# Attention stage of a four-stage block: x tiles asked for two tiles ahead, pair loops written out as eight straight-line tiles

## What is computed

```python
x = _layernorm(hidden_states)                       # (8, 1024, 256)
q, k, v = (x @ W.T + b for each of q, k, v)          # 16 heads of 16
attn_scores = einsum('bihd,bjhd->bhij', q, k) / 4
logits = (x @ rel_W[:, :256].T)[:, :, None] + (x @ rel_W[:, 256:].T)[:, None] + rel_b
bias = einsum('bijk,hk->bhij', softmax(logits), logical_bias)
attn_scores += sigmoid(x @ gate_W.T + gate_b) * bias
out = softmax(attn_scores) @ v
hidden_states + out @ Wo.T + bo
```

## Time and profile before

| | us |
|---|---|
| median of 3 runs | 6223.31 (6222.27 to 6227.41) |
| profiled execution, its own time | 6220.41 |
| its span, first to last instruction | 6218.6 |
| attention, from the first head's step of tile 0 to the last of tile 63 | 2943.24 |

### The profile page before, as it was taken

One profiled execution on the slowest core, in us unless ns is written; L12 is line 12 of the kernel. 1 busy time (PEld: TensorE's weight loads), 2 busy tenths in 40 slices (PEclk: granted clock), 3 DMA queues, 4 the chain that ended last, 5 costly groups with the idle time before them and its releaser, 6 DMA issues. The chain is left out here.

```text
span 6218.6 us, 125297 instructions
## 1 busy us (share of the span) xinstructions
PE 5465.2 (88%) x40162; PEld 3538.9 (57%) x40162; DVE 4684.7 (75%) x6099; ACT 4429.8 (71%) x7069; POOL 3649.6 (59%) x2010
## 2 busy tenths in 40 slices
PE   6888888888888888888699969999999979999999
PEld 4666666666666666655444435555555546666665
DVE  7888889889888888888799849999999952221221
ACT  5999989899898998999566668888888841111111
POOL 4777777777777777777300029999999950000000
PEclk8999999999999999999899979999999999999999
DMA  2121121211212121120155565555555541111110
GB/s 71 28 47 29 27 47 30 45 27 29 46 27 47 28 42 31 28 44 17 38 182 193 207 216 182 195 202 200 205 196 198 183 148 34 34 50 34 34 34 11
DMA packets 461188, 538.63 MB, mean 87 GB/s; under 512 B 237520, under 2 KB 337616, under 8 KB 460640
## 3 DMA queue, kind: packets, MB, share of 16 engines
q1 hardware_dynamic: 460640, 531.62, 27.4%
HBM read 370.17 MB, written 161.35 MB: 85 GB/s over the span
## 5 line engine op out<-in xcount | busy, mean ns | idle before, releaser
L502 DVE CUSTOM_DVE_ANT_0 srow<-srow,ps_s,cur 128x1024 f32<-128x1024 f32 x1024 | 1305.5, 1275 | 249.5 <-PE ps_s L650 174.9
L579 ACT ACTIVATE srow<-srow,nmax 128x1024 f32<-128x1024 f32 x1024 | 1192.1, 1164 | 201.5 <-DVE nmax L502 189.7
L588 ACT COPY AT<-ps_t 128x512 f32<-128x512 f32 x2048 | 1105.5, 598 | 61.6 <-PE ps_t L661 60.7
L661 PEld LDWEIGHTS ps_t<-ident,srow 128*128 128x128 f32 x8192 | 959.9, 143 | 279.5 <-ACT AT L588 87.8
L661 PE MATMUL ps_t<-ident,srow 128*128 128x128 f32 x8192 | 1102.5, 278 | 12.6 <-ACT AT L588 8.4
L1977 POOL TENSOR_TENSOR c_hc<-c_hs,c_cs 128x1024 f32<-128x1024 f32 x432 | 1009.9, 2366 | 64.7 <-DVE c_hs L2079 62.6
L491 DVE SCALAR_TENSOR_TENSOR srow<-ps_p,rho,R 128x1024 f32<-128x1024 f32 x768 | 976.7, 1272 | 7.8 <-PE ps_t L661 4.5
L650 PE MATMUL ps_s<-K,Q 96*128 96x512 bf16 x2048 | 629.2, 389 | 402.0 <-DVE nmax L502 313.9
L1938 PE MATMUL c_ps_y<-c_hc,c_ident 128*128 128x512 f32 x2048 | 944.7, 594 | 30.0 <-POOL c_hc L1977 17.1
L2079 DVE TENSOR_TENSOR_SCAN c_hs<-c_da,c_pd 128x1024 f32<-128x1024 f32 x384 | 859.7, 2274 | 56.3 <-PE c_pd L1929 55.1
L2022 ACT ACTIVATE c_sT<-c_dxT,c_bT 128x256 f32<-128x256 f32 x1536 | 668.4, 494 | 108.9 <-PE c_pd L1929 98.7
(11 more groups left out here) (257 smaller groups left out, 8258.3 us busy)
## 6 DMA issues: line engine op xcount, KB each, us to landing
c_cs<-bc_d SPq DMA_DIRECT2D x256, 512.0 KB, 4.3
c_bs<-bc_d SPq DMA_DIRECT2D x64, 512.0 KB, 6.6
Q<-parts_d SPq DMA_DIRECT2D x384, 64.0 KB, 2.2
parts_d<-parts SPq DMA_DIRECT2D x57, 384.0 KB, 3.3
K<-parts_d SPq DMA_DIRECT2D x168, 128.0 KB, 4.3
sz_d<-b_sz SPq DMA_DIRECT2D x16, 1024.0 KB, 7.2
xv_d<-b_xv SPq DMA_DIRECT2D x16, 1024.0 KB, 8.5
dt_d<-b_ab SPq DMA_DIRECT2D x16, 1024.0 KB, 4.2
```

Source lines behind the costliest of these rows:

```text
L502: nc.vector.tensor_tensor_reduce(r[:], r[:], ps_s[:], cur[k][:, h:h + 1], BIG, ALU.add, ALU.min, nmax[:, h % NROW:h % NROW + 1]).then_inc( ...
L579: nc.scalar.activation(r[:], r[:], ACT.Exp, scale=-1.0, bias=nmax[:, h % NROW:h % NROW + 1]).then_inc(e_ok, 1)
L588: nc.scalar.copy(AT[h % NAT][:, HG * half:HG * half + HG, :], ps_t[:, half]).then_inc(at_ok, 1)
L661: last = nc.tensor.transpose(ps_t[:, half, i, :], rows_sb[h % NROW][:, j * P:(j + 1) * P], ident[:])
```

## The change

SP asks for x tile t+10 in tile t instead of t+9, into the other slot, and one more tile (9) ahead of the first `body`. The last loads wrap round to tiles that nobody reads, one more than before, and a wait at the end covers it. In `run`, the two kinds of inner `Fori` become Python loops, so that the instructions of all eight tiles of a batch stand one after the other. The outer loop stays.

```diff
@@ run
-                with eng.Fori(1, NT // 2 - ends) as i:
+                for i in range(1, NT // 2 - ends):
                     for k in range(2):
                         body(eng, first + 2 * i + k, k, par, 2 * i + k, True, True, True, before=par)
...
-            with eng.Fori(1, NT // 2 - 1) as i:
+            for i in range(1, NT // 2 - 1):
                 for k in range(2):
                     body(eng, (B - 1) * NT + 2 * i + k, k, 1, 2 * i + k, False, True, True, before=1)
@@ block.sync
                 sp_first_keys(sp, 1)
                 sp_parts(sp, NT)
+                sp_x(sp, NT + 1, 1)
...
                 if pro:
-                    sp_x(sp, t + AHEAD, 1 - k)
+                    sp_x(sp, t + AHEAD + 1, k)
...
                 sp.wait_ge(st, 16 * TILES)
+                sp.wait_ge(x_in_s, 16 * (TILES + 2))
```

## The result

The change brings the median from 6223.6 us (four executions, one more than in the table of before) to 6144.65; the ratio is 0.9871, with a 95% interval of 0.9858 to 0.9885. One of the four executions after took 7937.86 us, at a mean granted clock of 0.648, and is in the median but not in the ratio; the other three took 6141.94 to 6145.12 us at 0.978 to 0.979. The profiled execution took 6144.19 us, against 6220.41 before.

A forecast was written before the change was run, and what follows sets the result against it. DVE and ACT nearly fill a regular attention tile (45.08 us), so only longer tiles' excess can go: 49.2 (x load) + 18.8 (inner loops) = 68.0 off 6220.4 gives 6152.4; median 2.9 above, 6155; range 6146 to 6180.

The forecast's parts named there:

- The x load: First tiles of batches 1 to 6: asking earlier removes DVE's six waits for x and gains 49.2 us.
- The 1.0 us left for tiles 24 and 40: Part of the 50.2 us excess not counted as gain, since the outer jump's stall and clock dip stay there.
- The inner jumps: 15 tiles behind an inner jump: writing the loops out removes their 22.1 us of excess.
- Rival (b): PE's stall comes at code boundaries anyhow, so writing loops out does not remove it: 6177, chance 0.05.
- the price of that can be read: Engines beside PE fetching straight code: 0.28 us in each of 12 more tiles, a cost of 3.3 us.
- the first two rows of the table: Gains forecast for attention: 49.2 us in first tiles of batches 1 to 6, 22.1 behind inner jumps.
- The median's distance to the profiled execution: Whole kernel: the median lies 2.9 us above the profiled execution, taking 6152.4 to the predicted 6155.
- Rival (d): More is won: new code costs nothing and outer jumps lose their tail; gain 77.4 us, 6146, chance 0.10.
- the outer jumps lose their tail: Part of the case that more is won: the 5.1 us at tiles 23 and 39 go too.
- The forecast's own range: 6149 to 6167, from 0 to 8.4 us for fetches and 0 to 7 for what stays in first tiles.
- (a): First tiles of batches: another wait, xr, store or K, replaces the x wait; 6180, chance 0.09.
- (c): Slower: straight code starves DVE or ACT, DVE stalling 2.89 us in each of 30 tiles; 6239, chance 0.02.

The follow-up runs named there:

- e3: The change with only PE's inner loops written out, loops kept on SP, POOL, DVE and ACT; 6148.12 us (one run).
- e4: The change with PE's inner loops kept and all other engines written out; 6168.1 us (one run).
- e2: The change with the x loads of before, so only the inner loops written out; 6193.79 us, ratio 0.9948 to the kernel before.
- e5: The change with inner loops written out on PE and POOL only, kept on SP, DVE and ACT; 6149.98 us (one run).
- e10: The change with inner loops kept on ACT and SP only; 6144.77 us (one run).
- e1: The change with the inner loops put back, so only the earlier x load; 6177.61 us, ratio 0.9923 to the kernel before.
- e6: The change with the outer loop written out as well, on every engine; 6133.39 us, ratio 0.9855 to the kernel before.
- e7: The kernel without any loops, but with the outer loop kept on DVE alone; 6142.73 us (one run).
- e8: The kernel without any loops, but with the outer loop kept on PE alone; 6144.22 us (one run).

## Why the prediction was right and wrong

- **The x load: right.** It waited for nothing, the six waits went, and no other wait took their place; the excess went whole, 50.3 us against 49.2. The store did close up behind Q as described, xr came when the store had landed, and landed 4.5 us ahead of its reader. The 1.0 us left for tiles 24 and 40 was 0.3 (90.38 us, against twice 45.03).
- **The inner jumps: right**, 23.2 us against 22.1. Rival (b) fell in e3 and e4: the stall is the jump's, and PE's. Of the stall, though, PE's lead hides 2.4 us of 3 and not half, and more than half of the 1.5 us comes with the low clock. The difference of 1.1 us is the base: the three of these tiles in batches 0 and 7 became constants and came out 0.1 to 0.2 us below it, the other twelve 0.05.
- **The step that failed** is "the price of that can be read: ... where these engines run code for the first time in the batch". The prediction took the 0.28 us of the second and fourth tiles as the price of straight code and charged 3.3 us for twelve more tiles of it. The fetches came exactly as forecast, 8 and 6 pieces in tiles 12 and 13 after the change:

```profile
q8 instruction: 8, 0.13, 0.6%
q14 instruction: 6, 0.05, 0.2%
```

  But they cost nothing (45.04 us a tile), and the 0.28 us was the price of having a loop on POOL and DVE near these tiles: it went with the loops (e2, e4, e5, e10). So the term had the wrong sign: +3.4 in place of -3.3, 6.7 of the 8.2 us by which the forecast of the profiled execution (6152.4) missed the 6144.19 measured. The others are 1.1 each in the first two rows of the table and 0.9 in the other 29 tiles, less 0.2 for tiles 23 and 39 and 1.5 for the rest of the span. That batch 0 had no such excess in its tile 3 was in the trace and should have spoken against it, since it runs new code too. It has a loop as well, so the loops' price is shown only by taking them away. That q8 carries PE's instructions and q14 those of the other engines is borne out by the same two tiles of e3 and e4: 8 and 1 pieces with PE alone straight, 10 and 6 with all but PE.
- **The median's distance to the profiled execution** was taken as 2.9 us, as before the change. After it the profiled execution lies 0.5 below the median, and is itself the middle one of 6141.94, 6144.19 and 6145.12. The distance is scatter, but it was carried into the centre of the range.
- **Rival (d)** came closest: 77.4 us of gain, 6146. It is right in its size and in "the new code costs nothing", and wrong in "the outer jumps lose their tail": they cost 5.3 us as before. The range ended at this rival's time and left nothing beyond it for terms that had been taken as fixed. The forecast's own range was mis-added too: its two bounds give 6151 to 6166, not 6149 to 6167.
- **Rivals (a) and (c)** were not seen: no wait for xr or K stands in the first tiles (POOL waited for xr once, 1.1 us, in tile 63). DVE's waits on its own stream grew from 54.8 us (89 times) to 65.1 (99), which by the prediction would have been a sign of being wrong. But they grew in batches 0 and 7, whose tiles became shorter, and the waits on PE at the same line fell from 174.9 to 143.1; in batches 1 to 6 each tile has one such wait of 0.2 us, apart from tiles 24 and 40.
- **The price of a jump.** The runs show 2.8 to 3.5 us of stall on PE for an inner jump, 4.1 to 5.3 for the outer one, and 2.1 to 4.3 on DVE for the outer one. By the figure of about 108 ns for a compare-and-branch (the Trainium skill, "Advanced Engine Details and Errata", Control Flow Timing) the 15 tiles would have stayed at 46.3 us, an estimate from that page; they fell to 44.9. What the Trainium skill, "Runtime: NRT & Kernel Launch", Instruction fetch mechanics, says of a taken branch, that its target has to be fetched first when it is out of the window, fits all of these stalls; that going straight on is mostly hidden fits too. Why the outer jump costs PE more than the inner one was not tried.

## What to carry to other kernels

Cut the profile into the rounds of the loop and compare their lengths: a load behind a block of slow ones in one queue, and the jumps of the engine that streams the most instructions, show as excess of single rounds, at their full price. A small excess in "new" code is not yet the price of new code; look for a round that is new and has none. Move first what is asked for behind the block, then write out the loops of the engines whose jump is seen. Find out engine by engine whose jump that is: at the inner loop here it was PE's alone, while at the outer loop PE's and DVE's lay over each other, and taking away one of them gained nothing. And take such prices from more than one profiled execution: how much of a stall shows depended on what the clock did behind it.

## What the runs showed of the hardware

- An inner jump back on PE cost 0.6, 1.5 or 3.1 us on the same stall of about 3 us, by how long PE's clock was at 1.2 GHz behind it: none, 3.4 or 6.8 us (e1). Which of the three it was changed from run to run of nearly the same code: 13 of 15 jumps had 3.4 us before, 6 of 15 in e1, 9 of 15 in e4.
- Straight code of some 14,800 PE instructions for two batches (7424 matmuls and 7424 weight loads) ran without one matmul waiting for PE's stream; PE fetched 8 pieces of 16 KB for two tiles straight and 10 in a round of the loop.
- With the loops gone and constants in place of register arithmetic, a tile was 0.17 us shorter on a program whose DVE and ACT are busy for 41 and 42 of 45 us (e6 against the change); most of it went with DVE's loop (a regular tile is at 44.99 in e7 and 44.89 in e8).
